# Attention with two denominator groups, a fifth accumulating DMA and earlier row-max tiles

## The reference

```python
h = layernorm(x) * (1 + ca) + sa
q = (h @ Wq.T)      # 32 heads of 32
k = (h @ Wk.T)      # 8 key/value heads of 32
v = (h @ Wv.T)
att = softmax(q k^T / sqrt(32), axis=-1)     # 4 query heads share one k and v head
y = att v
x = x + ga * (y @ Wo.T + bo)
h = layernorm(x) * (1 + cb) + sb
x = x + gb * ffn(h)                          # gate, up, silu, int8 rounding, down
```

## Time and profile before

| what | value |
|---|---|
| median of 3 runs | 3582.47 us (3580.29 to 3582.48) |
| the profiled execution's own time | 3583.01 us |
| its span, first to last instruction | 3581.2 us |
| granted TensorE clock, mean | 0.983 of 2.4 GHz |
| PE busy over the span | 3462.8 us (97%) |
| DVE busy | 2218.3 us (62%) |
| ACT busy | 1600.1 us (45%) |
| POOL busy | 1602.9 us (45%) |
| attention stage, from the trace | about 395 to 2052 us |

### The profile page before, as it was taken

How to read it: one execution, slowest core, us unless ns; L and a number is a source line. 1 busy time by engine, 2 the same in 40 slices (tenths; PEclk the granted TensorE clock), 3 DMA queues, 4 the chain that set the end, 5 groups by cost and what they waited for, 6 DMA issues and landing times. The chain is left out here.

```text
span 3581.2 us, 46156 instructions
## 1 busy us (share of the span) xinstructions
PE 3462.8 (97%) x17196; PEld 2314.1 (65%) x17196; DVE 2218.3 (62%) x3730; ACT 1600.1 (45%) x2990; POOL 1602.9 (45%) x701
## 2 busy tenths in 40 slices
PE   6999899999999999999999699799999999998998
PEld 4778455555555555555555288688888888887786
DVE  5545677777777777777777088444444444442727
ACT  3210466666666666666666433222222222213544
POOL 1111488989989899899889700000000000000010
PEclk8999899999999999999999899899999999999999
DMA  6662555656555555556554445611111111113212
GB/s 228 206 189 82 131 119 107 123 109 123 112 115 113 112 121 111 116 112 122 110 107 95 91 166 173 182 29 29 29 30 29 29 29 29 30 41 118 94 64 86
DMA packets 196090, 361.96 MB, mean 101 GB/s; under 512 B 41744, under 2 KB 122896, under 8 KB 175696
## 3 DMA queue, kind: packets, MB, share of 16 engines
q0 software_dynamic: 37120, 202.92, 24.9%
q1 hardware_dynamic: 156496, 154.69, 15.7%
q10 hardware_dynamic: 2304, 2.10, 0.2%
HBM read 162.13 MB, written 62.78 MB: 63 GB/s over the span
## 5 line engine op out<-in xcount | busy, mean ns | idle before, releaser
L872 DVE TENSOR_REDUCE att_chunk_max<-att_scores 128x1 f32<-128x512 f32 x1984 | 1212.9, 682 | 352.1 <-PE att_scores L940 352.1
L853 ACT ACTIVATE att_exp<-att_scores_T 128x512 f32<-128x512 f32 x2048 | 1049.5, 621 | 449.9 <-PE att_scores_T L954 441.8
L797 POOL TENSOR_TENSOR att_exp_pair<-att_exp 128x2048 f32<-128x2048 f32 x256 | 1199.7, 4737 | 62.8 <-ACT att_exp L853 62.3
L965 PE MATMUL att_y_acc<-att_exp,att_v_head 128*32 128x512 f32 x4096 | 499.0, 605 | 0.0
L1327 POOL DMA_DIRECT2D inter_scratch<-gu_inter x84 | 45.2, 538 | 882.6 <-DVE gu_inter L1270 882.6
L940 PE MATMUL att_scores<-att_kq,att_q_stack 96*128 96x512 f32 x768 | 327.3, 430 | 3.8 <-DMA att_q_stack<-q_scratch 2.4
L940 PE MATMUL att_scores<-att_k_stack,att_q_stack 96*128 96x512 f32 x768 | 325.0, 426 | 0.3
L954 PE MATMUL att_scores_T<-att_q_stack,att_k_stack 98*128 98x512 f32 x768 | 299.3, 412 | 2.4 <-ACT att_exp L853 2.3
L954 PE MATMUL att_scores_T<-att_q_stack,att_kq 98*128 98x512 f32 x768 | 296.4, 405 | 0.7 <-ACT att_exp L853 0.7
L1381 ACT ACTIVATE gu_magnitude<-gu_value 128x512 f32<-128x512 f32 x88 | 55.7, 633 | 516.7 <-DVE gu_value L1412 516.7
L1411 DVE TENSOR_TENSOR gu_rounded<-gu_up_acc,gu_rounded 128x512 f32<-128x512 f32 x88 | 60.9, 692 | 323.7 <-PE gu_up_acc L1446 323.7
(11 more groups left out here) (222 smaller groups left out, 6059.8 us busy)
## 6 DMA issues: line engine op xcount, KB each, us to landing
att_exp_pair<-att_exp_pair POOLq DMA_DIRECT2D x128, 1024.0 KB, 7.2
att_q_stack<-q_scratch SPq DMA_DIRECT2D x72, 256.0 KB, 5.8
shared_raw<-in_wd_t POOLq DMA_DIRECT2D x34, 256.0 KB, 3.3
qkv_x_tile<-in_x SPq DMA_DIRECT2D x16, 512.0 KB, 4.7
q_scratch<-qkv_qk_out_hi POOLq DMA_DIRECT2D x32, 256.0 KB, 3.1
q_scratch<-qkv_qk_out_lo POOLq DMA_DIRECT2D x32, 256.0 KB, 4.2
qkv_wqkv_raw<-in_wmod POOLq DMA_DIRECT2D x8, 1024.0 KB, 7.3
qkv_wmod<-in_wmod POOLq DMA_DIRECT2D x8, 1024.0 KB, 8.2
```

Source lines behind the costliest of these rows:

```text
L797: nc.gpsimd.tensor_tensor(ps[PAIR_SLOT[j]][:], pr[2 * j % NP][:], pr[(2 * j + 1) % NP][:], ALU.add).then_inc(pair_done, 1)
L853: nc.scalar.activation(pr[k % NP][:, h * NB:(h + 1) * NB], stp[bank(u, c, GH * k + h)][:], ACT.Exp, scale=INV_SQRT_DH).then_inc(exp_done, 1)
L872: nc.vector.reduce_max(cmax[c % 2][:, q:q + 1], turn_buffer(u, c, q)[:], AX.X).then_inc(sm_done, steps_done(u, q))
L965: ins = nc.tensor.matmul(yp[h * DH:(h + 1) * DH, :], vg[c // QB % 2][:, k, :], pr[k % NP][:, h * NB:(h + 1) * NB], start=(k == 0), stop=(k ...
```

## The change

A fifth accumulating DMA (number 4, slot 4 += slot 3) joins the group of pairs 4 to 5 with that of pairs 6 to 7 and, through number 3, pair 7. It is issued on POOL in the next unit, between pair 0 and pair 1, and waits for DMA 3 and for the quad sum. PE then needs two groups instead of three, in steps 0 and 8 instead of 0, 2 and 6. The copy of the denominators moves from step 6 to 8 and the reciprocal from step 9 to 11. Pair 3 now waits for DMA 4 instead of for PE's third group. The last unit has no DMA 3 and 4: PE sums four groups there, as soon as their pairs are ready.

TSTEP moves from 14 to 12 (14 stays for the first unit), so LEAD becomes 5: the transpose, the split and the stores of the maxima come two steps earlier, and each turn too. The first unit makes 20 turns of unit 2 in its last three steps (2, 8 and 10), where it made 12.

```diff
@@ -561,19 +561,20 @@
     NP, NS = 8, 5
     PAIRS = KT // 2
     PAIR_SLOT = (0, 1, 2, 3, 4, 1, 3, 2)
-    DMA_SUM = ((0, 1), (2, 3), (0, 2), (3, 2))
-    SUM_PAIRS = (1, 3, 3, 7)
+    DMA_SUM = ((0, 1), (2, 3), (0, 2), (3, 2), (4, 3))
+    SUM_PAIRS = (1, 3, 3, 7, 7)
     DMA_AFTER = {1: 0, 3: 1, 4: 2, 7: 3}
     QUAD_AFTER = 5
-    DEN_SLOT = (0, 4, 3)
+    DEN_SLOT = (0, 4)
     ND = len(DEN_SLOT)
-    DEN_AT = (0, 2, 6)
+    DEN_AT = (0, 8)
+    LAST_SLOT = (0, 4, 3, 2)
     RP = 8
-    DEN_COPY = 6
-    RECIP_AT = 9
+    DEN_COPY = 8
+    RECIP_AT = 11
     Y_AFTER = 5
     DW = GH * NB // P
-    TSTEP = 14
+    TSTEP, FIRST_TSTEP = 12, 14
     PER = NTURN // KT
     LEAD = KT - TSTEP + 1
     FIRST_TURNS, FIRST_LATE = 6, 12
@@ -638,14 +639,19 @@
 
             return 2 if c % BODY == 1 and i < 2 else NST
 
+        def tstep(u):
+
+            return FIRST_TSTEP if is_first(u) else TSTEP
+
         def turns(u, k):
 
             if is_first(u):
                 done = [min(max(0, FIRST_TURNS * i - FIRST_LATE), NTURN) for i in (k, k + 1)]
-                ahead = [(1, q) for q in range(*done)]
+                late = {KT - 3: (0, 2), KT - 2: (2, 10), KT - 1: (10, PER * LEAD)}.get(k, (0, 0))
+                ahead = [(1, q) for q in range(*done)] + [(2, q) for q in range(*late)]
             else:
                 ahead = [(1, q) for q in range(PER * (k + LEAD), PER * (k + LEAD + 1)) if q < NTURN]
-            ahead += [(2, q) for q in range(PER * (k + LEAD - KT), PER * (k + LEAD - KT + 1)) if q >= 0]
+                ahead += [(2, q) for q in range(PER * (k + LEAD - KT), PER * (k + LEAD - KT + 1)) if q >= 0]
             return [(n, q) for n, q in ahead if not beyond(u, n)]
 
         def units(eng, unit):
@@ -785,7 +791,8 @@
                     if u:
                         pool.wait_ge(dma_sum[3], u * 16)
                 elif j == 3:
-                    pool.wait_ge(den_done, 3 + u * ND)
+                    if u:
+                        pool.wait_ge(dma_sum[4], u * 16)
                 elif j == 4:
                     pool.wait_ge(den_done, 2 + u * ND)
                 elif j == 5:
@@ -803,6 +810,9 @@
                 if i == 2:
                     pool.wait_ge(dma_sum[0], 16 + u * 16)
                     pool.wait_ge(dma_sum[1], 16 + u * 16)
+                elif i == 4:
+                    pool.wait_ge(dma_sum[3], 16 + u * 16)
+                    pool.wait_ge(quad_done, u + 1)
                 pool.dma_start(ps[into][:], ps[other][:], accum_op=ALU.add).then_inc(dma_sum[i], 16)
 
             def quad_sum(u):
@@ -818,8 +828,10 @@
 
             def unit(u, c, g):
                 for j in range(PAIRS):
+                    if j == 1 and not is_first(u):
+                        sum_by_dma(u - 1, 4)
                     pair(u, j)
-                    if j in DMA_AFTER:
+                    if j in DMA_AFTER and not (beyond(u, 1) and j == PAIRS - 1):
                         sum_by_dma(u, DMA_AFTER[j])
                     if j == QUAD_AFTER:
                         quad_sum(u)
@@ vector, unit @@
-                    if k == TSTEP and not ahead and not beyond(u, 1):
+                    if k == tstep(u) and not ahead and not beyond(u, 1):
                         max_rows(u + 1, c + 1)
...
-                    if k == TSTEP - 2 and not beyond(u, 1):
+                    if k == tstep(u) - 2 and not beyond(u, 1):
                         row_max(u + 1, c + 1)
@@ -966,20 +978,34 @@
                                            pr[k % NP][:, h * NB:(h + 1) * NB], start=(k == 0), stop=(k == KT - 1))
                 ins.then_inc(pv_done, 1)
 
+            def ones_by(slot, first, last):
+
+                part = ps[slot]
+                for h in range(GH):
+                    ins = nc.tensor.matmul(dp[h * DH:(h + 1) * DH, :], ones[:], part[:, h * NB:(h + 1) * NB],
+                                           start=first, stop=last)
+                return ins
+
             def denominators(u, i):
 
                 if i == 0:
                     pe.wait_ge(dma_sum[2], 16 + u * 16)
                     pe.wait_ge(den_copied, u + 1)
-                elif i == 1:
-                    pe.wait_ge(quad_done, u + 1)
                 else:
-                    pe.wait_ge(dma_sum[3], 16 + u * 16)
-                part = ps[DEN_SLOT[i]]
-                for h in range(GH):
-                    ins = nc.tensor.matmul(dp[h * DH:(h + 1) * DH, :], ones[:], part[:, h * NB:(h + 1) * NB],
-                                           start=(i == 0), stop=(i == ND - 1))
-                ins.then_inc(den_done, 1)
+                    pe.wait_ge(dma_sum[4], 16 + u * 16)
+                ones_by(DEN_SLOT[i], i == 0, i == ND - 1).then_inc(den_done, 1)
+
+            def last_denominators(u):
+
+                pe.wait_ge(dma_sum[2], 16 + u * 16)
+                pe.wait_ge(den_copied, u + 1)
+                pe.wait_ge(quad_done, u + 1)
+                ones_by(LAST_SLOT[0], True, False)
+                ones_by(LAST_SLOT[1], False, False)
+                pe.wait_ge(pair_done, NP // 2 + 7 + u * PAIRS)
+                ones_by(LAST_SLOT[2], False, False)
+                pe.wait_ge(pair_done, NP // 2 + 8 + u * PAIRS)
+                ones_by(LAST_SLOT[3], False, True).then_inc(den_done, ND)
 
             def unit(u, c, g):
                 for k in range(KT):
@@ tensor, unit @@
-                    transposing = k == TSTEP and not beyond(u, 1)
+                    transposing = k == tstep(u) and not beyond(u, 1)
@@ tensor, after the units @@
-            for i in range(ND):
-                denominators(NU - 1, i)
+            last_denominators(NU - 1)
```

## The result

The changed kernel takes **3638.66 us** (median of 4 runs, 3634.11 to 3640.82) against 3581.85 for the kernel before in the same comparison (4 runs): a ratio of 1.0158, 95% interval 1.0140 to 1.0175. It is slower by 57 us. The forecast was 3660, range 3618 to 3700, slower with a chance of 0.88.

What follows compares the result with a forecast made beforehand. POOL's own cycle, 50.0 us growing to 53.7, was taken as the bound with the change. Over the stage +81, first unit +3.5, last unit -7.3 sum to +77 on 3583: 3660 us, range 3618 to 3700.

Steps and rivals of the forecast that it cites:

- What bounds the kernel: POOL over one unit: its own cycle is 50.0 us with 1 us to spare, though busy only 45.4 us.
- The fifth DMA: On POOL between pair 0 and pair 1: its wait for DMA 3 adds 3.71 us, making the cycle 53.7 us.
- PE's saved 0.86 us: PE's third group, removed from 30 units: 0.86 us each, 26 us less if PE stays the bound; otherwise it becomes waiting.
- over the stage: POOL's 30 cycles of 53.7 us less the 1529.7 us they took before: +81 us.
- The low bound of 7.54 us: Shortest DMA 1 to DMA 2, used for DMA 3 to DMA 4: 2.95 us more per cycle, sum down to 3637.
- Who waits: PE's second group in step 8 waits for DMA 4, 3.6 us per unit; no second wait in step 0.
- a wait in step 0: Sign at PE's first group of a unit: if PE waits there as well, the forecast's size is off.
- the slower rival: PE's clock falls to 1.2 GHz in its new wait; three stretches per unit cost 45 us more, 3705 us; chance 0.11.
- Steps moved on SP: Denominators' copy two steps later, maxima's stores two earlier: stores go out at about the same time, cost nothing.
- First unit: DVE makes 8 more maxima there at 0.61 us each: between 0 and +4.9 us, taken as +3.5.
- Last unit: PE's last group starts with the end of pair 7 instead of waiting for DMA 3: -7.3 us.
- the faster rival: PE stays the bound, DMA 4's wait vanishes and its issue is free: 3553 us; chance 0.08.

Runs made afterwards that it cites:

- the padded run: Kernel before with one more small product per unit on POOL and a wait for its end: 3598.32 us, ratio 1.0047.
- that half: Kernel before with only the second half of the change: transpose in step 12, turns five steps ahead, 20 late turns in the first unit: 3586.43 us, ratio 1.0015.
- the run with DMA 2 late in the kernel before: Kernel before with DMA 2 issued after pair 5 instead of after pair 4: 3634.75 us, ratio 1.0150.
- the denominators' half alone: Changed kernel with transpose back in step 14 and turns three steps ahead; two groups, fifth DMA and copy in step 8 kept: 3633.49 us, ratio 1.0144.
- The changed kernel with DMA 2 late: Changed kernel with DMA 2 issued after pair 5 instead of after pair 4: 3562.34 us, ratio 0.9947.
- the run with the fifth DMA late: Changed kernel with only the fifth DMA moved from before pair 1 to behind it: 3586.21 us, ratio 1.0013.

## Why the prediction was right, and where it was off

*What bounds the kernel.* POOL's own cycle of 50.0 us and its 1 us of room were read nearly right; by the padded run the room was 0.8. That DMA issues do not count as busy was wrong for this profile: the 45.4 us of the earlier trace rows hold four of them, and without them it is 42.7. The cycle was read from the timeline and does not depend on it.

*The fifth DMA.* The mechanism and its place held: an uncovered wait between pair 0 and pair 1, POOL as the bound, PE's saved 0.86 us turned into waiting. The **size of the term "over the stage" was too large**: +81 us, and POOL's cycles give 56.3 us for 29 of them and about 2.2 us for the last (52.2 us to the last group, against 57.3 - 7.3 = 50.0), 58.5 us. Two numbers in it were off. From DMA 3 to DMA 4 I took the 8.30 us of DMA 1 to DMA 2 in one cycle; in the changed kernel most of these gaps are 7.5 us, with waits of 73.6 / 30 = 2.45 us on average instead of 2.79. And I kept the wait ahead of DMA 2 at its 3.01 us; it fell to 74.4 / 30 = 2.48 us. Together 0.9 us per unit, which covers the 0.74 us by which 53.7 missed 52.96. In the traces the median landing of DMA 1, for which DMA 2 waits, went from 7.8 to 7.0 us, and that of DMA 2 from 7.0 to 7.9. A likely reason, only argued: before, SP's four loads of the denominators (1093.76) run beside DMA 1 (1092.20), and now (1496.20) beside DMA 2 (1496.55). The low bound of 7.54 us, taken from unit 31, was the typical value: the median from DMA 3 to DMA 4 is 7.50.

*Who waits.* PE was to wait 3.6 us in step 8 of each unit, and nowhere else. It waited 1.7 us per unit, mostly in step 0, and lost about 1 us per unit more to the clock, at half in 12 stretches of 61 us; the two together are 2.8 us, as much as 52.96 has over the prediction's 50.13 of work. The prediction had named a wait in step 0 as a sign that its size was off. That PE loses its clock in the new wait was the slower rival's mechanism; it came, and as the prediction says of one stretch or two it stayed hidden, since it was less than one per unit.

*Steps moved on SP.* Costed at nothing. For the changed kernel this held (+6.2 us for that half, all of it in the first unit), but the reason did not: the stores do not go out and land as they did. They go out 1.4 us after DMA 2 instead of 6.8, and their median landing went from 1.9 to 6.3 us. The prediction named no price for the case that they come late; the run with DMA 2 late in the kernel before shows it, 54 us.

*First unit.* +3.5 us taken, +4.4 us at DMA 3 of unit 1, +6.2 us as a run by itself: within the range of 0 to 4.9 us by the one, above it by the other. The +4.4 hold two parts: with the denominators' half alone DMA 3 of unit 1 comes at 507.66, 1.5 us earlier than before (a gain for which the prediction had put down nothing), and the 8 extra turns add 513.61 - 507.66 = 6.0 us.

*Last unit.* -7.3 us taken, -7.4 us measured.

*The rivals.* The formula of the Trainium skill ("DMA: Bandwidth & Descriptors", section "Anatomy of one DMA"), by which 1 MB lands in an estimated 4.4 us and the wait would not exist, is not borne out: no accumulating DMA landed under 6.9 us in any run whose landings were read. The step from it to the faster rival does not hold either. Even with no wait at all, the prediction's own pieces put 2 x 5.78 us where 10.37 stood, a cycle of 50.0 + 1.2 = 51.2 us: an estimate of 3585 us, no difference, and not 3553. The changed kernel with DMA 2 late came near that rival's time, 3562 us, but by another way, since the fifth DMA's wait is still in it and another was covered.

## What to carry to other kernels

In this kernel, an engine that also issues DMAs had to be judged by its own cycle, work and in-order waits together, with the waits for other engines taken off, and not by its busy time: 45.4 us busy in a unit of 51.0 hid a cycle of 50.0. Elsewhere this is worth looking at first. A step added to such a queue cost its issue plus what was left of the wait in front of it, and where in the list it stands decided: one DMA issued one pair later was worth 76 us here. Before a large transfer is moved, look which small one it will meet and who starts on that one; the same move cost 54 us where it met the stores that the next unit begins with.

## What the hardware showed that was not expected

- Small stores beside a large transfer: the 8 KB stores of the maxima took 1.9 us to land in the kernel before, 3.6 us where a 1 MB accumulating DMA was issued 3.6 us ahead of them, and 6.3 us in the changed kernel, where DMA 2 is issued 1.4 us ahead. In the kernel before, too, DMA 2 is under way, but was issued 6.8 us ahead. The issue on SP grew as well, from 0.59 to 1.39 us.
- Two accumulating DMAs close together: with the fifth DMA behind pair 1, DMA 0 is issued 0.6 us after it (median) and lands in 11.8 us, where it took 7.1 in the changed kernel; the first of the two lands in 7.3.
- A DMA issue on POOL whose waits were met began 0.36 us before the add ahead of it had ended (1033.56 against 1033.92 in the run with the fifth DMA late).
- The granted clock fell to 1.2 GHz beside waits of PE of only 1.8 to 5.0 us, 12 times in units 2 to 29 of the changed kernel, though not at every such wait, and in none of these units before, where PE was busy for 1448.83 of 1450 us. With DMA 2 late in the kernel before it fell 9 times beside waits of only 1.2 to 2.4 us.
